# Adding x to the result by accumulating transfers instead of on TensorE and VectorE

## The reference

```
xn = _layernorm(x, axis=-1)
s = _L0_attn_ref(xn, ...)          # delta-rule linear attention, 4 heads, gated, times Wo
g = _silu(_L0_ffn_ref(xn, ...))    # each token through one of 8 experts: 256 -> 1024 -> 256
x = x + s * g
```

## Time and profile before

| | |
|---|---|
| median of 3 runs | 796.69 us (796.59 to 797.21) |
| the profiled execution: its time | 798.03 us |
| the profiled execution: its span | 796.2 us |
| granted TensorE clock in it | 0.998 |
| TensorE busy, share of the span | 97% |
| VectorE, ScalarE, GpSimd busy | 66%, 44%, 49% |
| software queue q0 (GpSimd's transfers) | 3.9% of the 16 DMA engines |
| hardware queue q1 (SyncE's transfers) | 35.8% |

### The profile page before, as it was taken

How to read it: one execution, slowest core, us unless ns; L and a number is a source line. 1 busy time by engine, 2 the same in 40 slices (tenths; PEclk the granted TensorE clock), 3 DMA queues, 4 the chain that set the end, 5 groups by cost and what they waited for, 6 DMA issues and landing times.

```text
span 796.2 us, 22202 instructions
## 1 busy us (share of the span) xinstructions
PE 769.3 (97%) x9002; PEld 650.8 (82%) x9002; DVE 524.7 (66%) x1151; ACT 349.5 (44%) x762; POOL 388.5 (49%) x407
## 2 busy tenths in 40 slices
PE   6969999999999999999999999999999999999977
PEld 5957888888888888888888888888787887879854
DVE  6686565665755557465575655776777777677786
ACT  4823434444344444444444343444444444435432
POOL 3725373544625456263552635446464646445341
PEclk9999999999999999999999999999999999999999
DMA  9608634533344343432534335314042333323075
GB/s 303 214 2 326 231 126 171 188 114 132 126 184 165 114 155 130 182 139 114 182 129 167 129 114 204 149 34 181 34 152 88 128 113 121 128 107 114 9 245 199
DMA packets 37748, 116.25 MB, mean 146 GB/s; under 512 B 3664, under 2 KB 24400, under 8 KB 27664
## 3 DMA queue, kind: packets, MB, share of 16 engines
q1 hardware_dynamic: 33904, 104.62, 35.8%
q0 software_dynamic: 3744, 10.23, 3.9%
HBM read 101.33 MB, written 13.50 MB: 144 GB/s over the span
## 4 chain that ended last, share of the span: by engine, by line
PE 84%; DVE 6%; POOL 4%; issue 4%; DMA 1%; another core or an unknown queue 0%; ACT 0%; DVEq 0%; POOLq 0%; SPq 0%
PE bank L504 18%; PE bank L515 16%; PE bank L548 6%; PE bank L580 6%; PE bank L533 6%; PE bank L480 4%; PE bank L478 4%; PE bank L479 3%; PE bank L722 2%; PE bank L629 2%; PE bank L620 2%; PE bank L638 2%; PE bank L435 2%; PE bank L560 2%; POOL XTl L2392 1%
## 5 line engine op out<-in xcount | busy, mean ns | idle before, releaser
L515 PE MATMUL bank<-wts,hT 128*128 128x256 f32 x624 | 171.2, 393 | 0.0
L504 PE MATMUL bank<-xsT,wts 128*128 128x128 f32 x1248 | 166.2, 281 | 0.1
L504 PEld LDWEIGHTS bank<-xsT,wts 128*128 128x128 f32 x1248 | 150.8, 192 | 11.7 <-issue 11.7
L2392 POOL TENSOR_TENSOR XTl<-f_t,XTh 128x512 f16<-128x512 f32 x32 | 39.6, 1241 | 151.6 <-DVE XTh L1695 151.5
L1755 DVE TENSOR_TENSOR Pm<-bank,lvl_mask 128x256 f16<-128x256 f32 x180 | 68.2, 419 | 65.9 <-PE bank L620 62.5
L515 PEld LDWEIGHTS bank<-wts,hT 128*128 128x128 f32 x624 | 105.3, 191 | 7.3
L1766 DVE TENSOR_TENSOR M<-bank,M 128x256 f16<-128x256 f32 x180 | 68.9, 419 | 51.0 <-PE bank L629 50.6
L1201 ACT CAST Z<-bank 128x256 f16<-128x256 f32 x180 | 59.4, 376 | 91.3 <-PE bank L638 91.2
L1146 ACT ACTIVATE hT<-bank 128x512 f32<-128x512 f32 x78 | 46.7, 599 | 50.9 <-PE bank L504 50.9
L580 PE MATMUL bank<-wvg_sb,xT 128*128 128x512 f32 x128 | 63.4, 618 | 0.0
L548 PE MATMUL bank<-xT,wq_sb 128*128 128x128 f32 x512 | 63.1, 276 | 0.0
(11 more groups left out here) (247 smaller groups left out, 1948.0 us busy)
## 6 DMA issues: line engine op xcount, KB each, us to landing
wts<-in_fc SPq DMA_DIRECT2D x39, 1024.0 KB
wts<-in_pj SPq DMA_DIRECT2D x39, 1024.0 KB
wts<-in_x SPq DMA_DIRECT2D x10, 512.0 KB, 7.6
wts<-y_d SPq DMA_DIRECT2D x4, 1024.0 KB, 9.5
out_x<-wts SPq DMA_DIRECT2D x16, 256.0 KB, 2.3
xn_d<-wts SPq DMA_DIRECT2D x3, 1024.0 KB, 4.4
x_first<-in_x SPq DMA_DIRECT2D x4, 512.0 KB, 17.4
wts<-in_x SPq DMA_DIRECT2D x4, 256.0 KB, 3.4
```

Source lines behind the costliest of these rows:

```text
L504: ins = pe.matmul(psum[bank[n]][:, (c % 4) * P:(c % 4 + 1) * P], fcw[r][:, k, c * P:(c + 1) * P], xsT[:, k, :], start=(k == 0), stop=(k == ...
L515: ins = pe.matmul(psum[bank[0]][:, 0:D], hT[:, c, :], pjw[r][:, c, :], start=(c == 0), stop=(c == HC - 1))
L2392: pool.tensor_tensor(h4(XT[1][a % 2], b), h4(f32_t, b), h4(XT[0][a % 2], b), ALU.subtract).then_inc(Xl_ok[b], 1)
```

## The change: what it does

The additions of x on TensorE, ScalarE and VectorE are gone, and with them both loads of x for them. In place of the first load, SyncE copies x into the result in DRAM, 4 transfers of 1 MB from DRAM to DRAM. In the last pass only `weigh(c)` is left, and then GpSimd issues for each chunk one transfer that adds the product in SBUF to the result in DRAM (`accum_op=ALU.add`, 256 KB, 256 rows of 1 KB). The first of them waits until the four copies have landed. SyncE's 16 stores are gone. The lists of calls in `tail()` are new for every engine; those of `ramp()` and the steps are as before.

```
+                for k in range(GROUPS):
+                    r = slice(B * N * k // GROUPS, B * N * (k + 1) // GROUPS)
+                    sp.dma_start(out.rearrange("b n d -> (b n) d")[r], x.rearrange("b n d -> (b n) d")[r]).then_inc(x_out, 16)
...
-                for c in range(NCH):
-                    sp.wait_ge(out_act if c in ON_PE else out_dve, added(c))
-                    sp.dma_start(o_v[c], chunk_of(c)).then_inc(o_out, 16)
...
-                def add_x(c):
-                    n = added(c)
-                    if n == 1:
-                        At(pe, NT - 1).on(y_ok)
-                    if n > 2:
-                        pe.wait_ge(out_act, n - 2)
-                    pe.wait_ge(xf_in[c // (NCH // 2)], 16 * B * GROUPS // 2)
-                    pe.matmul(sum_bank(c), ident[:], x_of(c), start=True, stop=False)
-                    pe.wait_ge(ys_ok, c + 1)
-                    pe.matmul(sum_bank(c), ident[:], chunk_of(c), start=False, stop=True).then_inc(sum_ok, 1)
...
-                def keep_sum(c):
-                    act.wait_ge(sum_ok, SUM_FROM + added(c))
-                    act.copy(chunk_of(c), sum_bank(c)).then_inc(out_act, 1)
...
-                def add_x(c):
-                    dve.wait_ge(ys_ok, c + 1)
-                    dve.wait_ge(xf_in[c // (NCH // 2)], 16 * B * GROUPS // 2)
-                    dve.tensor_tensor(chunk_of(c), chunk_of(c), x_of(c), ALU.add).then_inc(out_dve, 1)
...
+                def add_x(c):
+
+                    if c == 0:
+                        pool.wait_ge(x_out, 16 * GROUPS)
+                    pool.wait_ge(ys_ok, c + 1)
+                    pool.dma_start(o_v[c], chunk_of(c), accum_op=ALU.add).then_inc(o_out, 16)
```

More of the change, by code:

```diff
@@ L315, in chunk_of @@
             return yf[:, c].rearrange("p (b d) -> p b d", b=B)
-        def x_of(c):
-            return (x_first[:, c] if c < NCH // 2 else x_last[:, c - NCH // 2]).rearrange("p (b d) -> p b d", b=B)
+        o_v = out.rearrange("b (c p) d -> c p b d", p=P)
         def part_of(c):
@@ L1057, in tail @@
                     F(14)
+                    experts(1)
                     T(15, 1)
-                    VG(15, 0)
[L1060 to L1067, removed]
+                    experts(3)
+                    L(15, 2)
+                    Zc(14)
+                    experts(2)
+                    Dm(15, 2)
+                    experts(1)
+                    U(14)
+                    T(15, 2)
+                    VG(15, 0)
                     L(15, 3)
@@ L2200, in tail @@
                     R_h(14)
+                    Pm_(15, 2, 0)
+                    Pm_(15, 2, 1)
                     R_l(14)
-                    Pm_(15, 2, 1)
-                    Pm_(15, 2, 0)
-                    P_h(15, 0)
-                    v(15, 0)
                     dM(15, 2, 0)
@@ L2209, in tail @@
                     U_l(14)
+                    Pm_(15, 3, 0)
+                    v(15, 0)
+                    Pm_(15, 3, 1)
                     gate_(15, 0)
-                    Pm_(15, 3, 1)
-                    Pm_(15, 3, 0)
                     dM(15, 3, 0)
                     dM(15, 3, 1)
+                    og_(14)
                     oss_(14)
-                    og_(14)
                     Pm_(15, 4, 0)
@@ L2515, in tail @@
                 def tail():
+                    rows(36)
+                    rows(37)
                     orn_(12)
-                    rows(36)
                     krn_(14)
+                    ogm(12)
                     k_l(14, 0)
-                    ogm(12)
                     k_l(14, 1)
-                    rows(37)
-                    rows(38)
                     X_l(14, 0)
-                    X_l(14, 1)
                     ImM_(13, 0)
                     ImM_(13, 1)
+                    X_l(14, 1)
+                    P_l(14, 1)
                     P_l(14, 0)
-                    P_l(14, 1)
+                    root_(14)
+                    rows(38)
+                    krn_(15)
                     gate_y(34)
-                    root_(14)
-                    krn_(15)
                     k_l(15, 1)
@@ L2535, in tail @@
                     orn_(13)
+                    gate_y(35)
                     ogm(13)
+                    X_l(15, 0)
                     send_y(34)
                     X_l(15, 1)
-                    X_l(15, 0)
-                    gate_y(35)
+                    send_y(35)
+                    gate_y(36)
+                    send_y(36)
                     ImM_(14, 0)
                     ImM_(14, 1)
-                    send_y(35)
-                    gate_y(36)
-                    P_l(15, 0)
                     gate_y(37)
-                    send_y(36)
                     send_y(37)
+                    P_l(15, 1)
                     gate_y(38)
                     send_y(38)
+                    P_l(15, 0)
                     orn_(14)
                     ogm(14)
+                    add_x(0)
+                    add_x(1)
+                    add_x(2)
                     ImM_(15, 0)
                     ImM_(15, 1)
-                    P_l(15, 1)
+                    add_x(3)
+                    add_x(4)
+                    add_x(5)
+                    add_x(6)
+                    add_x(7)
+                    add_x(8)
+                    add_x(9)
                     orn_(15)
                     ogm(15)
+                    add_x(10)
+                    add_x(11)
+                    add_x(12)
+                    add_x(13)
+                    add_x(14)
+                    add_x(15)
                 ramp()
```

364 lines of the change are left out of this document (163 added, 201 removed).

## The result

The changed kernel takes 802.95 us (802.09 to 803.43, 4 runs), the kernel before 796.67 (796.59 to 797.21, 4 runs): a ratio of 1.0079, 95% interval 1.0067 to 1.0090. The forecast was 799.6, within 793 to 812, with 0.67 on slower. Sign and range held, but +2.9 us became +6.3.

What follows compares the result with a forecast made beforehand. TensorE's chunk-15 chain bounded the kernel before; its 5.1 us saving would lie under DMA transfers: 759.75 + 37.6 + 1.75 = 799.1 against 796.2, +2.9 us, so 796.7 + 2.9 = 799.6 us, range 793 to 812.

Steps and rivals of the forecast that it cites:

- GpSimd's queue: Tail on GpSimd: issue pitch 1.34 us, orn(15) at 780.75, norm done 784.7, last issue 791.4 to 792.7, later than the chain.
- the early load: Tail: the load of y_d starts 2.7 us sooner, at 758.5, takes 12.0 us, and lets weigh(0) go at 764.1.
- the price of a transfer: Each 256 KB accumulating transfer occupies the DMA engines 1.6 us, between bounds of 0.75 and 2.4.
- the DMA engines' backlog: Tail: 37.6 us of DMA work from 759.75 ends at 797.4; 7 us of backlog cover GpSimd's 3.8 us without issues.
- the first case: Two passes per accumulating transfer, DMA bound: 799.6 us, own range 797 to 803, chance 0.40.
- The rival of VectorE's wait: Tail: without an earlier y_d load, weigh(0) holds back Pm_, chain 1.9 us later; 0.10 together with cheap moving at pitch 1.34.
- The rival with a pitch of 2.38: GpSimd's issue cost goes with rows: end about 811, +14.7 us; within the dear case, 803 to 820, chance 0.25.
- two passes: An accumulating transfer costs two passes at 0.80 us per 256 KB, 1.6 us, because two reads come through each engine.
- Chain: Recurrent chain of chunk 15: without the sums of x, 4.4 us gained ahead of the last multiply, last weigh ending at 788.4.
- TensorE loses 8 x 1.76 = 14.1 us: Last pass: TensorE sheds eight add_x of 1.76 us each, mostly in waits, so the chain gains only 4.4 us.
- Behind the last byte: End of the kernel: 1.75 us from the DMA engines' end at 797.4 to the end at 799.1.
- The rival of the other sign: Cheap transfers, price below about 1.4 us and pitch below 1.3: -3.4 us, 793.3; case 792 to 795, chance 0.20.

Runs made afterwards that it cites:

- the second run: The changed kernel with plain stores from GpSimd in place of the accumulating transfers (result lacks x): ratio 1.0062 to the kernel before, 802.73 us against 797.83.
- the half-and-half kernel: Changed kernel, but GpSimd's accumulating transfers only for chunks 0 to 7, VectorE adds and SyncE stores 8 to 15, 130 small matmuls hold TensorE's clock: 0.9964, repeat 0.9962.
- clock kept: The changed kernel with 130 small unread matmuls where TensorE waits in the tail: ratio 1.0076 to the kernel before.
- old lists: The new way of adding x in the kernel before's order of work, seven accumulating transfers ahead of orn(15), nine behind ogm(15): ratio 1.0132 to the kernel before.
- no copy: The changed kernel without the four copies of x to the result in DRAM (result lacks x): ratio 1.0095 to the kernel before.

## Why the prediction held, and where its size was off

**What held and what was luck.** GpSimd's queue, the early load and the price of a transfer came out as forecast. But the reason given for the slower end was the DMA engines' backlog, and that isn't what the runs show. The forecast's own path ends with the landing at 796.7, 0.9 us later than the last landing before, which is 0.1%: no change; and with cheap transfers, the second run, the kernel was still 0.6% slower. What makes it slower is a term that the sum didn't have, GpSimd's closing drain. That the time still fell into the first case's 797 to 803 is luck.

**Order and early load.** Right to within a microsecond: load of `y_d` issued at 758.15 (758.5), `weigh(0)` at 763.86 (764.1), and GpSimd's queue as above. The rival of VectorE's wait didn't occur.

**Issue on GpSimd.** Taken 1.34, measured 1.24; 256 rows are issued at a smaller pitch than 128 indirect ones, though not as fast as plain stores (0.73 in the second run, under my lower bound of 1.0). The rival with a pitch of 2.38 falls.

**Price of a transfer.** Taken 1.6. The engines worked from 759.4 (759.75) to 796.2; less the 12.0 of the load that is 24.8 us for 16, 1.55 each. So the number for two passes was right, and the engines' end (797.4 forecast) came 1.2 us sooner; that two reads through each engine are the reason is not shown by any run. The plain store in the second run occupied the engines for 0.28 x 43 / 16 = 0.75 us, the lower bound. The rate isn't constant, though: 190 GB/s in 776 to 786 and 157 behind it.

**Chain.** The waits for sums did go, but `ogT_(15)` (1.12 instead of 0.60) and `wo(15)` (3.57 instead of 1.89) gave 2.2 of the 4.4 us back to the clock. The step "TensorE loses 8 x 1.76 = 14.1 us" counted those sums as pure cost. They also held the clock. It made no difference to the time of this kernel, since the saving lies under GpSimd's queue and its end; the half-and-half kernel shows its price.

**Behind the last byte: this step failed.** "Behind the last byte: a gather lands 3.2 us after issue, of which 1.04 is issue and 0.40 moving, so 1.75. End: 799.1." The landing came 0.5 us behind the last busy engine, at 796.7, and the end is not the landing. GpSimd's closing drain was left out of the sum, with 4.0 us. From the forecast end: 799.1 - 1.2 (engines) - 1.2 (landing) + 4.0 (drain) = 800.7, the end in the trace. Two terms that were too large hid 2.4 us of the 4.0 that were missing. The trace of before shows this drain, but it ended 3.7 us ahead of the program, and no step asked what would be later than it once GpSimd worked last.

**The rival of the other sign** gave 793.3 for cheap transfers. It couldn't have come about. With stores of 0.75 us and a pitch of 0.73, both under the values below which it was to decide, the second run was still 0.6% slower than the kernel before. By the rival's own times the sixteenth transfer would be issued from 788.9, and with 0.73 of issue and the 7.8 us that the drain took behind it in that run, the end is 797.4: no gain. The same missing term is why its chance of 0.20 was too high. **The early copy** was hidden, as forecast: its four transfers were issued from 66.8 us and landed after 22.2 us (median) and 26.0 at most, with 421 GB/s up to 90 us and 241 for ten more, while TensorE was busy throughout:

```profile
65.00:90.00 25.00, 24.96 (x265) 21.93 (x264) 13.86 (x32) 11.79 (x25) 9.16 (x10) 1.00 1.06 421
90.00:100.00 10.00, 10.00 (x111) 7.65 (x110) 6.59 (x15) 3.49 (x9) 6.71 (x7) 1.00 0.70 241
```

## What to carry to other kernels

Look in the trace at how each engine closes, not only at its last instruction. A cheap last transfer or a memset on GpSimd can cost more than all that it replaces: hand GpSimd the early share of such work and let it end well before the others (its drain ended 6.4 to 9.8 us behind its last instruction in these runs). Before taking work off TensorE in a tail that waits, ask what its clock does without it, and price what is left at both levels.

## What the runs showed of the hardware

- **GpSimd's drain** ends 6.4 to 7.4 us behind its last operation where that is no transfer (kernel before and eight runs), 7.8 behind the end of its last plain store's issue, and 3.8 to 4.0 behind the last landing where 16 accumulating transfers are in the queue (changed kernel, clock kept, old lists, no copy). In the run without the copy both readings fit, 7.9 behind the last issue and 3.9 behind the landing. That it waits for its own transfers fits all this but isn't shown by itself; what it does in the rest stays open.
- **An accumulating transfer** of 256 KB in rows of 1 KB occupied the engines 1.79 us against 0.75, with 4400 packets against 1328, and landed 8.1 us after issue against 3.3. The Trainium skill, page "DMA: Bandwidth & Descriptors", section "Anatomy of one DMA — SWDGE (gpsimd) path", gives 2.0 us plus the bytes over 436 GB/s, by which I estimate 2.6 us. The plain store is near it, with 2.5 us at the shortest and 3.3 in the median; the accumulating one isn't, with 5.3 to 10.4, and the measurement decides.
- **GpSimd and VectorE hold each other up.** Beside GpSimd's additions `R_l` took 1.64 us instead of 0.69; beside VectorE's uninterrupted run `ogm(15)` took 6.62 instead of 1.12. The Trainium skill, page "SBUF — State Buffer", section "Who interferes with whom", says that a VectorE operation with two inputs in SBUF contends with a GpSimd operation that reads SBUF, and that whichever comes second is blocked. The traces agree in part. Where `ogm(15)` took 1.20 us, VectorE's five products beside it took 3.93 us instead of 3.09, so that VectorE lost 0.84 us. Where `ogm(15)` took 6.62, those products took 3.09, and it ended at 787.58, 0.9 us behind the last of VectorE's additions: it was held up for a row of instructions, not for one. What decides between the two stays open.
